# Winograd's seven products for queries and keys in a fused transformer block on Trainium2

## The reference

```python
ada = (cond @ ada_w + ada_b)[:, None, :]          # shift1, scale1, gate1, shift2, scale2, gate2
x1 = _ln(x) * (1.0 + scale1) + shift1
qkv = (x1 @ qkv_w + qkv_b).reshape(Bc, Tc, 3, H, DH)      # 16 heads of 128
q, k, v = (qkv[:, :, 0], qkv[:, :, 1], qkv[:, :, 2])
attn = softmax(einsum('bthd,bshd->bhts', q, k) * DH ** -0.5)
attn_out = einsum('bhts,bshd->bthd', attn, v).reshape(Bc, Tc, INNER) @ out_w + out_b
x = x + gate1 * attn_out
x = x + gate2 * (gelu((_ln(x) * (1.0 + scale2) + shift2) @ ffn_w1 + ffn_b1) @ ffn_w2 + ffn_b2)
out = x0 + (rms_norm(relu(x @ w1) ** 2) @ w2)             # w1, w2 ternary; x0 is the input
```

## Time and profile before

| | us |
|---|---|
| Median of 3 runs | 360.06 |
| Lowest, highest | 358.48, 360.09 |
| The profiled execution's own time | 358.39 |
| Its span, first to last instruction | 356.6 |
| PE busy in the span | 348.0 (98%) |
| DVE, ACT, POOL busy | 210.0 (59%), 201.2 (56%), 107.5 (30%) |
| Mean granted clock of TensorE | 0.997 |

### The profile page before, as it was taken

The page is one execution under the profiler, slowest core; times in us unless marked ns, Lnnn a source line. Parts: engine busy times, 40 slices in busy tenths (PEclk is TensorE's granted clock), DMA queues, the critical chain, the costliest instruction groups (busy, mean ns, idle before and its releaser), DMA issues.

```text
span 356.6 us, 5788 instructions
## 1 busy us (share of the span) xinstructions
PE 348.0 (98%) x1998; PEld 300.7 (84%) x1998; DVE 210.0 (59%) x397; ACT 201.2 (56%) x524; POOL 107.5 (30%) x97
## 2 busy tenths in 40 slices
PE   8999899999999999999999999999999999999995
PEld 7788788888888888888888888888887888788875
DVE  5762347436535743643574354557875876677796
ACT  2675454545355454546555444656479645975593
...
PEclk9999999999999999999999999999999999999998
...
GB/s 177 367 202 85 4 118 61 0 0 2 119 0 118 59 0 0 0 118 3 115 0 0 0 0 118 2 0 61 1 2 0 1 2 0 2 0 0 3 29 88
DMA packets 12321, 16.52 MB, mean 46 GB/s; under 512 B 704, under 2 KB 8976, under 8 KB 12304
## 3 DMA queue, kind: packets, MB, share of 16 engines
...
q10 hardware_dynamic: 144, 0.13, 0.1%
HBM read 15.25 MB, written 1.05 MB: 46 GB/s over the span
## 4 chain that ended last, share of the span: by engine, by line
PE 72%; issue 20%; DVE 4%; ACT 1%; DMA 1%; POOL 1%; POOLq 0%; ACTq 0%; DVEq 0%
PE bank L1010 17%; PE bank L1012 16%; PE bank L1011 16%; PE bank L1058 8%; PE bank L1039 8%; PE bank L1047 4%; DMA xt<-in_x_dram 1%; PE bank L1128 1%; DVE stats L670 1%; POOL rstd L344 1%; DVE hid_lo L736 1%; PE bank L1149 0%; DVE yT L762 0%; ACT o_hi L460 0%; DVE prob L690 0%
## 5 line engine op out<-in xcount | busy, mean ns | idle before, releaser
L349 POOL TENSOR_TENSOR prob<-prob,rinv 128x512 f32<-128x512 f32 x32 | 33.3, 1042 | 148.8 <-DVE rinv L826 148.8
L495 ACT ACTIVATE prob<-bank,nbias 128x128 f32<-128x128 f32 x128 | 45.3, 366 | 40.3 <-DVE nbias L814 40.3
L811 DVE TENSOR_REDUCE negmax<-bank 128x4 f32<-128x512 f32 x32 | 22.1, 690 | 74.1 <-PE bank L1039 74.1
L1010 PE MATMUL bank<-x_hi,wqk_hi 128*128 128x512 f32 x126 | 52.5, 417 | 0.0
L1012 PE MATMUL bank<-x_hi,wqk_lo 128*128 128x512 f32 x126 | 49.6, 394 | 0.0
L1011 PE MATMUL bank<-x_lo,wqk_hi 128*128 128x512 f32 x126 | 49.2, 390 | 0.0
L460 ACT ACTIVATE o_hi<-bank,bias 128x512 fp32r<-128x512 f32 x32 | 22.0, 688 | 38.3 <-PE bank L1058 38.3
L464 ACT ACTIVATE vals<-bank 128x512 f32<-128x512 f32 x32 | 19.0, 597 | 36.5 <-PE bank L1012 35.6
L1058 PEld LDWEIGHTS bank<-probT,vals 128*128 128x128 f32 x256 | 33.5, 191 | 2.5
L744 DVE TENSOR_SCALAR kT<-bank,bias 128x512 f32<-128x512 f32 x32 | 24.0, 751 | 19.2 <-PE bank L1012 19.1
L1039 PE MATMUL bank<-kT,qT 128*128 128x128 f32 x256 | 33.9, 275 | 1.0 <-DVE ada L852 1.0
...
## 6 DMA issues: line engine op xcount, KB each, us to landing
...
```

The lines of the kernel that those rows point to most:

```text
L349: nc.gpsimd.tensor_tensor(e, e, rinv[:, j % 2, :].unsqueeze(2).broadcast_to([P, SQ, P]), ALU.mult).then_inc(norm_done, 1)
L495: e = nc.scalar.activation(prob[:, j % 2, s, :], bank[BS][:, s * P:(s + 1) * P], ACT.Exp, bias=nbias[:, j % 2, s:s + 1], scale=SCALE, accu ...
L811: nc.vector.tensor_reduce(negmax[:, j % 2, :], bank[BS][:, :].rearrange("p (s t) -> p s t", s=SQ), axis=AX.X, op=ALU.max, negate=True).the ...
L1010: nc.tensor.matmul(dst, ah, bh, start=start and n == 0, stop=False)
```

## The change

Seen as 2x2 blocks, a head's weights (rows: q and k; columns: the two halves of D) times the tokens (rows: the two halves of D; columns: the two quads) are eight block products. For 12 of 16 heads they become Winograd's form of Strassen's seven, with sums of weight blocks (`ws`) and of token blocks (`xc`) as operands, each split into `_hi` and `_lo` like the others. P1 and P2 give q of quad 0; P1+P6 is `u2`, +P7 is `u3`, +P4 is k of quad 0, all in the one bank BQ, which ACT copies out at each step (`copy_p1`, `copy_u2`, `copy_u3`, `pair_k0`); P5+`u3` is k of quad 1 and P5+P3+`u2` q of quad 1 (bank BE; DVE's `pair_k1`, `pair_q1`).

- One unit (a pair unit, j = 4, 0, 1, 2) computes all of q and k of one head, for both quads; q and k of quad 1 wait in `q1T`, `k1T`. Heads 0 to 2 of the first group and head 3 of the last keep the eight products, ahead of the loop and behind it.
- The other units (j = 3, 5, 6, 7) have the values' blocks: 4, 2, 1 and 1.
- POOL makes the weight sums (`weight_sums`: per group four instructions on 128x384 and four on 128x128) and their `_lo` (128x512 per head); ACT their `_hi` (128x512 per head). Each stands one to two units ahead of its use. DVE makes the token sums once, ahead of the loop (4 instructions on 128x512, 2 on 128x1024).
- A head's output has two buffers by the parity of the unit (`head_output`). On DVE `o_lo_part` now stands first in a unit, ahead of `negmax`.
- In the last group the `_hi` and `_lo` of the first feed-forward weights go to units 2 to 5, one piece each, where units 3 and 4 had two each.

The diff at its core:

```diff
+        xc = nc.alloc_sbuf_tensor_at("xc", [P, 4, TQ], F32, offset=w1_lo_at)
...
+        ws = nc.alloc_sbuf_tensor_at("ws", [P, 4, HG * P], F32, offset=w2_lo_at)
...
+        q1T = nc.alloc_sbuf_tensor_at("q1T", [P, HG, TQ], F32, offset=pairs_at)
+        k1T = nc.alloc_sbuf_tensor_at("k1T", [P, HG, TQ], F32, offset=pairs_at + HG * TQ * 4)
...
-        V_AT = {1: (4, 5), 2: (6, 7), 5: (0, 1), 6: (2, 3)}
-        W1_AT = {3: (0, 1), 4: (2, 3)}
-        W2_AT = {2: 0, 3: 1, 6: 2, 7: 3}
+        BE = BO + 1
+        PAIR_AT = {4: 0, 0: 1, 1: 2, 2: 3}
+        V_AT = {3: ((4, BQ), (5, BK), (6, BE), (7, BQ)), 5: ((0, BQ), (1, BK)), 6: ((2, BQ),), 7: ((3, BK),)}
+        V_LAST = {3: ((4, BQ), (5, BK)), 4: ((6, BE),), 5: ((7, BE),)}
+        WS_AT = {3: 0, 5: 1, 6: 2, 7: 3}
+        W1_AT = {2: 0, 3: 1, 4: 2, 5: 3}
+        W2_AT = {3: 0, 4: 1, 6: 2, 7: 3}
...
-            return (o2_hi, o2_lo) if isinstance(i, int) and i == NU - 2 else (o_hi, o_lo)
+        def head_output(j):
+            return (o2_hi, o2_lo) if j % 2 else (o_hi, o_lo)
...
+            def weight_sums(G, a0, a1, n):
+                s = slice(a0 * P, a1 * P)
+                nc.gpsimd.tensor_tensor(ws[:, 0, s], raw_qk[:, 2, s], raw_qk[:, 3, s], ALU.add).then_inc(ws_raw, 1)
+                nc.gpsimd.tensor_tensor(ws[:, 2, s], raw_qk[:, 0, s], raw_qk[:, 2, s], ALU.subtract).then_inc(ws_raw, 1)
+                pool.wait_ge(ws_raw, n + 1)
+                nc.gpsimd.tensor_tensor(ws[:, 1, s], ws[:, 0, s], raw_qk[:, 0, s], ALU.subtract).then_inc(ws_raw, 1)
+                pool.wait_ge(ws_raw, n + 3)
+                nc.gpsimd.tensor_tensor(ws[:, 3, s], raw_qk[:, 1, s], ws[:, 1, s], ALU.subtract).then_inc(ws_raw, 1)
...
+                if j == 4 and not last:
+                    for k in range(KD):
+                        wv_lo_part(k, KD * G + KD + k + 1)
                 normalise(UG * G + j, j)
...
+                if j == 2:
+                    wqk_lo_part(0, HG * G + HG + 1)
+                    pool.wait_ge(p1_mm, pair(G, 3))
+                    weight_sums(G + 1, 0, 3, 8 * G + 4)
                 if j == 5:
-                    wqk_lo_part(0, HG * G + HG + 1)
-                    wqk_lo_part(1, HG * G + HG + 2)
-                if j == 6:
-                    wqk_lo_part(2, HG * G + HG + 3)
+                    pool.wait_ge(p3_mm, pair(G, 3))
+                    weight_sums(G + 1, 3, 4, 8 * G + 8)
+                if j in (5, 6, 7):
+                    wqk_lo_part(WS_AT[j], HG * G + HG + WS_AT[j] + 1)
+                if j in WS_AT:
+                    ws_lo_part(G + 1, WS_AT[j])
...
+                if pair_unit:
+                    copy_p1(*pair_head(G, j))
                 act.wait_ge(nb_done, i + 1)
-                for s in range(SQ):
-                    e = nc.scalar.activation(prob[:, j % 2, s, :], bank[BS][:, s * P:(s + 1) * P], ACT.Exp,
-                                             bias=nbias[:, j % 2, s:s + 1], scale=SCALE,
-                                             accum_out=rowsum[:, j % 2, s:s + 1])
-                e.then_inc(exp_done, 1)
-                if more:
-                    G1, j1 = (G, j + 1) if j < UG - 1 else (G + 1, 0)
-                    keep_q(G1, j1)
-                if j == 0:
-                    wqk_hi_part(3, 32 * G + 32)
+                exps(i, j, range(2))
+                if pair_unit:
+                    copy_u2(*pair_head(G, j))
+                exps(i, j, range(2, SQ))
...
+                if not last:
+                    if j in (5, 6, 7):
+                        wqk_hi_part(WS_AT[j], 32 * G + 64)
+                    if j in WS_AT:
+                        ws_hi_part(G + 1, WS_AT[j])
+                if pair_unit:
+                    copy_u3(*pair_head(G, j))
+                vs = (V_LAST if last else V_AT).get(j, ())
+                for b, src in vs[:2]:
+                    keep_v(b, v_count(G, b), src)
+                o_hi_part(*before(G, j))
+                for b, src in vs[2:]:
+                    keep_v(b, v_count(G, b), src)
+                if pair_unit:
+                    pair_k0(*pair_head(G, j))
...
+            def pair_q0(G, a):
+                dve.wait_ge(p1_cp, pair(G, a))
+                dve.wait_ge(p2_mm, pair(G, a))
+                joined(qT[:, :], bank[BK][:, :], HG * G + QB + a, p1, q0_done)
+            def pair_k1(G, a):
+                dve.wait_ge(u3_cp, pair(G, a))
+                dve.wait_ge(p5_mm, pair(G, a))
+                joined(k1T[:, a, :], bank[BE][:, :], HG * G + KB + a, u3[:, :], k1_done)
+            def pair_q1(G, a):
+                dve.wait_ge(p3_mm, pair(G, a))
+                joined(q1T[:, a, :], bank[BE][:, :], HG * G + QB + a, u2, q1_done)
...
+            def pair_p1(G, a):
+                pe.wait_ge(wqk_l, head(G, a) + 1)
+                product(BQ, "raw", 0, a, "raw", (0, 0), start=True).then_inc(p1_mm, 1)
+            def pair_p2(G, a):
+                product(BK, "raw", 1, a, "raw", (1, 0), start=True).then_inc(p2_mm, 1)
+            def pair_p6(G, a):
+                pe.wait_ge(ws_l, pair(G, a))
+                pe.wait_ge(p1_cp, pair(G, a))
+                product(BQ, "sum", 1, a, "sum", 1).then_inc(p6_mm, 1)
+            def pair_p5(G, a):
+                pe.wait_ge(q1_done, head(G, a))
+                pe.wait_ge(k1_done, head(G, a))
+                product(BE, "sum", 0, a, "sum", 0, start=True).then_inc(p5_mm, 1)
+            def pair_p7(G, a):
+                pe.wait_ge(u2_cp, pair(G, a))
+                product(BQ, "sum", 2, a, "sum", 2).then_inc(p7_mm, 1)
+            def pair_p4(G, a):
+                pe.wait_ge(u3_cp, pair(G, a))
+                product(BQ, "raw", 3, a, "sum", 3).then_inc(p4_mm, 1)
+            def pair_p3(G, a):
+                pe.wait_ge(k1_done, head(G, a) + 1)
+                product(BE, "sum", 3, a, "raw", (1, 1)).then_inc(p3_mm, 1)
...
+            def pair_unit(G, j):
+                i, (g, a) = UG * G + j, pair_head(G, j)
+                scores(G, j)
+                if j == 4:
+                    pe.wait_ge(v_done, v_count(G, 7))
+                if j == 0:
+                    pe.wait_ge(v_done, v_count(G - 1, 3))
+                pair_p1(g, a)
+                transpose_p(i - 1, (j - 1) % 2)
+                pair_p2(g, a)
+                pair_p6(g, a)
+                pair_p5(g, a)
+                out_half(*before(G, j, 2), 0)
+                pair_p7(g, a)
+                pv(*before(G, j, 1))
+                pair_p4(g, a)
+                out_half(*before(G, j, 2), 1)
+                pair_p3(g, a)
+            def value_unit(G, j):
+                i, VG = UG * G + j, G if j == 3 else G + 1
+                scores(G, j)
+                transpose_p(i - 1, (j - 1) % 2)
+                if j == 3:
+                    pe.wait_ge(q1_done, head(G, 3) + 1)
+                if j == 5:
+                    pe.wait_ge(q0_done, head(G + 1, 0) + 1)
+                    pe.wait_ge(k0_done, head(G + 1, 0) + 1)
+                if j > 5:
+                    pe.wait_ge(v_done, v_count(G, j - 6))
+                first, *others = V_AT[j]
+                v_block(VG, *first)
+                if others:
+                    v_block(VG, *others.pop(0))
+                out_product(*before(G, j, 2))
+                pv(*before(G, j, 1))
+                for b, dst in others:
+                    if b == 7:
+                        pe.wait_ge(v_done, v_count(G, 4))
+                    v_block(VG, b, dst)
...
```

More of the change, by code:

```diff
@@ new lines, in keep_qk1, with joined @@
+            def keep_qk1(a, G, count, q_src, k_src):
+                dve.wait_ge(q_mm, count)
+                biased(q1T[:, a, :], bank[q_src][:, :], HG * G + QB + a, q1_done)
+                dve.wait_ge(k_mm, count)
+                biased(k1T[:, a, :], bank[k_src][:, :], HG * G + KB + a, k1_done)
+            def joined(dst, src, at, part, done):
+                nc.vector.scalar_tensor_tensor(out=dst, in0=src, scalar=bias[:, bass.ds(at, 1)], in1=part,
+                                               op0=ALU.add, op1=ALU.add).then_inc(done, 1)
@@ L802, in add_residual, with unit @@
                 m.then_inc(xr_done, 1)
-            def unit(G, j, vs, more, last=False):
+            def unit(G, j, last=False):
                 i = UG * G + j
-                first = isinstance(i, int) and i == 0
+                first, second = (isinstance(i, int) and i == n for n in range(2))
+                pair_unit = j in PAIR_AT and not last and not first and not second
                 end = last and j >= UG - 2
-                if end:
+                if not first and not second:
                     o_lo_part(*before(G, j, 2))
@@ L814, in unit @@
                 nc.vector.tensor_scalar(nbias[:, j % 2, :], negmax[:, j % 2, :], SCALE, None, ALU.mult).then_inc(nb_done, 1)
-                if (not isinstance(i, int) or i >= 2) and not end:
-                    o_lo_part(*before(G, j, 2))
                 if not first and not end:
```

(32 more changed lines are left out.)

361 lines of the change are left out of this document (215 added, 146 removed).

## The result

The changed kernel takes **360.84 us** (median of 17 runs, 360.77 to 360.99), the kernel before 360.04 (17 runs, 358.43 to 360.13): ratio 1.0035, 95% interval 1.0024 to 1.0046. It is 0.8 us slower in the median, where 1.9 us faster was forecast. The profiled executions are further apart: 360.88 against 358.39 us, spans of 359.1 and 356.6. The kernel before has two groups of runs, 358.3 to 358.6 and 359.7 to 360.2 us, and its profile fell in the lower one; what parts them is read under the last experiment. The traces thus compare the changed kernel with the lower group, by their spans: **+2.5 us**.

What follows compares the result with a forecast made beforehand. PE, busy 98% of the span, was taken as the bound: -8.2 us for 36 matmuls, +5.0 for waits in three rounds, +1.3 in the last group, -1.9 in all, from 360.06 to 358.1 us; range 353.5 to 362.0.

Steps and rivals of the forecast that it cites:

- a matmul taken out is worth its place: PE in the loop: 36 matmuls fewer at 0.228 us each save 8.2 us, 2.74 a round.
- The units' own times: PE's time without waits: pair unit 8.40 us, unit 3 9.09, unit 5 6.35, units 6 and 7 4.98 each.
- The ring: Units 5, 6, 7, 0: ACT's tail in one unit delays the next's softmax; 1.1 us a round, 0.7 without POOL's hold.
- nbias(6) held: Unit 6 in the loop: nbias on DVE waits for POOL's running instruction, ending at 3.1 us in place of 2.6.
- The last group's signs over nbias(6): Last group: POOL's ternary signs, 2.13 us, run until 5.0 of unit 6, while nbias wants to go at 3.7.
- The nearest row is the plain copy: 0.07: Pair units: P4 waits 0.07 us for u3's copy, 0.22 if it starts like o_hi; taken as 0.3 a round.
- Units 3 and 4, "I take 0.2": Block 7 waits 0 to 0.5 us for block 4's copy, taken as 0.2; with P1's 0.07, 0.27 a round.
- Ahead of the loop ... I take 0: Before the loop: token sums' _lo ready about 0.5 us after PE's last matmul, where it already waits 1.0; cost 0.
- The last group, 1.3: Last group: signs over nbias(6), last scores about 0.9 us late, o_lo 0.4 more; bounds 0.2 and 2.0, taken 1.3.
- the gain is just eaten: Rival, chance 0.20: fewer matmuls but as much waiting for copies; P4 at 0.22, units 3 and 4 at 0.6; 360.9 us.
- The base: Profiled execution 358.39 us becomes 356.5; the median of the runs is 1.7 above it, so 360.06 - 1.9 = 358.1 us.

Runs made afterwards that it cites:

- the last experiment: The kernel before with one edit, nbias made by ACT in place of VectorE: 360.02 us, ratio 1.0005 to the kernel before.
- experiment 4: Changed kernel with P2 issued twice in each of the 12 pair units, so the 36 matmuls come back: 368.65 us.
- experiment 9: As experiment 8, but P4 back at its place and P7 one matmul earlier, inside the first half of the output product: 351.59 us.
- experiment 1: Changed kernel with nbias made by ACT just ahead of the exponentials, in place of VectorE behind negmax: 356.62 us.
- experiment 7: Changed kernel with the last group's ternary signs and values on POOL at the end of unit 7, not in units 5 and 6: 360.46 us.
- experiment 3: Changed kernel with ACT's _hi of the weight sums in unit 3 behind the copies of blocks 4 and 5 and o_hi: 359.49 us.
- experiment 8: Changed kernel with nbias on ACT, P1 waiting for less, P4 later, sums' _hi later, banks exchanged, token-sum wait moved, last group's second compare ahead of reciprocal: 352.76 us.

## Why the prediction was wrong

**What held.** PE is the bound and a matmul taken out is worth its place (8.2 forecast, 7.8 by experiment 4). The units' own times, 8.40, 9.09, 6.35 and 4.98: experiment 9 has 8.40, 9.09, 6.35 and 4.99. The ring: 1.1 us a round forecast and measured, 0.4 and 0.7 in units 7 and 0 against 0.33 and 0.74; nbias(6) held, by experiment 1. That the sum came out is in part luck: by the prediction 0.4 of it was POOL's hold and 0.7 the durations, by experiment 1 it is 0.8 and 0.3. The last group's signs over nbias(6), by experiments 1 and 7. The Trainium skill (SBUF — State Buffer, section SBUF: two separate sides) says that a VectorE instruction with two SBUF inputs and a GpSimd one that reads SBUF exclude each other too. The trace of experiment 7 agrees: `hid_lo` took 2.01 us beside POOL's signs where it takes 0.69 alone.

**What failed** is the size of the waits: two terms of the round were taken below the middle of their bounds, one wait was taken at nothing, and two more weren't walked. Each is a few tenths to a us, and the sum missed by 4.4 us on a base of 358.4:

- *"The nearest row is the plain copy: 0.07".* P4's wait is 0.15. The copy of u3 starts 0.25 behind the last matmul of P7, between the plain copy's 0.20 and o_hi's 0.35. And P4's place was put 0.89 behind pv's start; it is 0.81 when a 512-column matmul follows, as the trace of before had it, from 128.57 to the line below. +0.3 a round.
- *Units 3 and 4, "I take 0.2".* The 128x384 sums take 1.00 to 1.02 each, not 0.8 to 0.95; the wait was near the top of the range given (0.47 of 0.5; experiment 3). P1 behind block 7 is 0.2, not 0.07: the copy comes at 0.86 of unit 4, and P1's place is again at 0.81, not 0.89. +0.4 a round.
- *Unit 2* was not walked: nbias(2) takes 0.58 (170.22 to 170.80) and ends with POOL's ternary values (170.77), and P7 waits; with nbias on ACT the unit is back at 8.55. +0.15 a round.
- *"Ahead of the loop ... I take 0".* 0.8. The `_lo` of the token sums was ready 1.2 after PE's last matmul (42.66 to 43.85), not 0.5, and PE's wait grew from 1.0 to 1.6. It ran beside POOL's `wo_lo`, which is the likely cause, not a shown one.
- *The last group, 1.3.* 2.5, of which 1.1 is unit 5's. The wait of its transposes was missed: nbias held 0.3, and normalise beside the compare, 1.93 us. That the two exclude each other is read from the trace; the edit that parted them (in experiment 8) only moved the cost.

The line of before:

```profile
129.38 0.48 PE L1010 MATMUL bank<-wv_hi,x_hi 128*128 128x512 f32 x1
```

The terms of the round make 2.5 over three rounds, and 2.5 + 0.8 + 1.2 = 4.5, the whole miss. The rival *the gain is just eaten* named the first two mechanisms and their sizes (P4 at 0.22, units 3 and 4 at 0.6) and gave 360.9 us. That it hit the median is luck: it lacked the other 2.4 us of waits, was 0.2 a round too high in the two that it had, and added a base that doesn't hold, as follows.

**The base.** The forecast was made against a profiled execution and moved to the median by adding 1.7. That step assumed that the change leaves the difference alone. It doesn't: in two of three runs the kernel before loses 1.6 us near the loop's start, by the clock as far as the last experiment tells, and no run of the changed kernel, which has more matmuls at that place, shows such a loss. Medians show +0.8 because +2.4 against the lower group meets -1.6. What of the start's new order keeps the clock up was not tried apart.
